# Attention with one key head: early 32-query blocks trade places, outputs take high heads first

## What is computed

```python
xn = layernorm(x, g_in)                                  # x: 64 x 128 x 512
q = heads(xn @ Wq) * 64 ** -0.5                          # 16 heads of 64
k, v = split(xn @ Wkv)                                   # one head of 64
sim = q @ [null_k, k].T + [null_bias, bias]              # 128 x 129 per head
sim = where(causal and mask, sim, -big)
out = softmax(sim) @ [null_v, v]                         # 128 x 64 per head
x + layernorm(concat(out) @ Wo, g_out)
```

## Time and profile before

| | |
|---|---|
| median of 3 runs | 1065.65 us (1062.91 to 1068.68) |
| the profiled execution | 1064.88 us |
| its span | 1063.0 us |
| busy: PE, PEld | 1029.5 us (97%), 902.9 us (85%) |
| busy: DVE, ACT, POOL | 765.8 us (72%), 661.2 us (62%), 828.9 us (78%) |
| TensorE's clock, mean | 0.989 of full |
| chain of work that ended last | PE 89%; projections 38%, outputs 33%, scores 9%, values 9% |

### The profile page before, as it was taken

One profiled execution on the slowest core, in us unless ns is written; L12 is line 12 of the kernel. 1 busy time (PEld: TensorE's weight loads), 2 busy tenths in 40 slices (PEclk: granted clock), 3 DMA queues, 4 the chain that ended last, 5 costly groups with the idle time before them and its releaser, 6 DMA issues.

```text
span 1063.0 us, 42980 instructions
## 1 busy us (share of the span) xinstructions
PE 1029.5 (97%) x14254; PEld 902.9 (85%) x14254; DVE 765.8 (72%) x3513; ACT 661.2 (62%) x2620; POOL 828.9 (78%) x1488
## 2 busy tenths in 40 slices
PE   6789999999999999999999999999999999999986
PEld 6678898888888888888888888888888889889875
DVE  4777777777777777786777787776777777777663
ACT  5655675666675665675665676565676565666552
POOL 2867887778878778878778788788788778787775
PEclk8999999999999999999999999999999999999998
DMA  7312222232222222222223122223222223121101
GB/s 213 124 34 86 77 81 89 67 94 76 63 85 82 74 87 73 68 84 85 76 82 91 50 87 84 86 70 89 62 78 85 83 73 93 54 84 59 50 25 60
DMA packets 90013, 84.01 MB, mean 79 GB/s; under 512 B 21568, under 2 KB 64064, under 8 KB 89792
## 3 DMA queue, kind: packets, MB, share of 16 engines
q1 hardware_dynamic: 88336, 81.03, 25.3%
q10 hardware_dynamic: 1456, 0.04, 0.1%
HBM read 40.11 MB, written 16.78 MB: 54 GB/s over the span
## 4 chain that ended last, share of the span: by engine, by line
PE 89%; issue 2%; POOL 2%; ACT 2%; DVE 1%; POOLq 0%; DVEq 0%; ACTq 0%
PE ps_proj L500 38%; PE ps_pv L488 33%; PE ps_s L452 9%; PE ps_pv L477 9%; ACT exp_bot L914 1%; POOL w_nrm L1112 1%; ACT exp_top L914 1%; POOL y_out L1156 0%; POOL y_nrm L1152 0%; DVE logit_bot L608 0%; DVE o_lo L630 0%; POOL bias_b L1103 0%; ACT xn L942 0%; POOL small L1138 0%; DVE wt L624 0%
## 5 line engine op out<-in xcount | busy, mean ns | idle before, releaser
L914 ACT ACTIVATE exp_bot<-logit_bot,neg_max 128x129 f32<-128x129 f32 x512 | 201.6, 399 | 252.0 <-DVE neg_max L608 223.0
L1103 POOL TENSOR_TENSOR bias_b<-bias_c,mask_add 128x256 f32<-128x256 f32 (+1 forms) x512 | 291.9, 599 | 45.3 <-DVE neg_max L608 45.2
L500 PE MATMUL ps_proj<-xt_hi,wq_hi 128*128 128x256 f32 x1024 | 302.5, 295 | 7.5 <-DVE q_sb L690 6.0
L500 PE MATMUL ps_proj<-xt_lo,wq_hi 128*128 128x256 f32 x1024 | 288.6, 282 | 0.9 <-issue 0.9
L500 PE MATMUL ps_proj<-xt_hi,wq_lo 128*128 128x256 f32 x1024 | 288.6, 282 | 0.0
L608 DVE CUSTOM_DVE_ANT_0 logit_bot<-ps_s,bias_b 128x128 f32<-128x128 f32 x512 | 128.3, 288 | 180.1 <-PE ps_s L452 162.4
L500 PEld LDWEIGHTS ps_proj<-xt_hi,wq_hi 128*128 128x128 f32 x1024 | 193.3, 189 | 24.9 <-issue 13.0
L1112 POOL TENSOR_TENSOR w_nrm<-exp_bot,w_inv 128x256 f32<-128x256 f32 x256 | 156.9, 613 | 65.2 <-DVE w_inv L617 65.2
L488 PE MATMUL ps_pv<-wo_hi,o_hi 128*128 128x512 f32 x488 | 199.0, 408 | 1.2 <-DVE o_lo L630 1.2
L488 PE MATMUL ps_pv<-wo_lo,o_hi 128*128 128x512 f32 x488 | 193.5, 397 | 0.0
L500 PEld LDWEIGHTS ps_proj<-xt_hi,wq_lo 128*128 128x128 f32 x1024 | 193.4, 189 | 0.0
(11 more groups left out here) (94 smaller groups left out, 1778.6 us busy)
## 6 DMA issues: line engine op xcount, KB each, us to landing
x_in<-in_x_dram SPq DMA_DIRECT2D x32, 512.0 KB, 4.1
x_res<-in_x_dram SPq DMA_DIRECT2D x64, 256.0 KB, 2.9
out_dram<-y_out SPq DMA_DIRECT2D x64, 256.0 KB, 2.1
x_split<-xn SPq DMA_DIRECT2D x480, 32.0 KB, 1.9
v_rep<-v_raw SPq DMA_DIRECT2D x256, 32.0 KB, 1.9
w_raw<-in_L_cond_Wq_dram SPq DMA_DIRECT2D x4, 512.0 KB, 11.7
w_raw<-in_L_cond_Wo_dram SPq DMA_DIRECT2D x4, 512.0 KB, 5.2
mask_u<-in_mask_BxS_bk_dram SPq DMA_DIRECT2D x31, 32.0 KB, 3.7
```

The source lines that it names most:

```text
L500: mm = pe.matmul(ps[:, 0:TOK], w[:, k, cols], xt[:, slot, k], start=(j == 0), stop=(j == len(todo) - 1))
L914: ins = nc.scalar.activation(out_[:, s, j], in_[:, s, j], ACT.Exp, bias=neg_max[:, s, k:k + 1], scale=-1.0, accum_out=w_sum[:, s, k:k + 1])
L1103: ins = nc.gpsimd.tensor_tensor(out_, bias, key_mask, ALU.add)
```

## The change

**Blocks trade places.** The tokens of a batch get a new order on chip: block 1 (tokens 32 to 63), block 0, block 2, block 3. TensorE's turning of x becomes a matrix product with placing, an identity whose first two column blocks are exchanged; split_x writes to PLACED[a]. Keys, queries and all that follows are then in this order, so in the early half the even row groups hold tokens 32 to 63 and the odd ones 0 to 31. The early products that need two key blocks move to the even row groups: ITEMS becomes five and five. The masks and the bias follow: mask_of writes two pieces, a second mask causal_early is built, make_bias reads a raw copy of the bias (loaded into the q_sb slot of the second group) and writes bias_c in exchanged order, in four calls of five operations in place of two of four; VectorE's first copy to that q_sb slot waits until all are done. The bias comes in 12 DMAs in place of 8, and every residual load and every store becomes three DMAs of 32, 32 and 64 rows in place of one.

**Outputs.** In each half the eight products with o_hi come first, then the four with o_lo. The half starts when two o_hi and one o_lo of it are made (the bank must be free), and waits for its second o_lo ahead of the four last products.

**Warm-up and layout.** The 30 transposes become three fp32 products of the identity with itself repeated four times, 512 columns wide. A tensor of 32 bytes per partition that nothing uses, home, is allocated ahead of Wo; placing (512 bytes) lies ahead of Wq.

```diff
-WARM = 30
+WARM = 3
+PLACED = (1, 0, 2, 3)
 ITEMS = (
-    [(1, 0), (1, 1), (1, 2), (0, 0)],
-    [(1, 0), (1, 1), (1, 2), (1, 3), (0, 0), (0, 1)],
+    [(1, 0), (1, 1), (1, 2), (0, 0), (0, 1)],
+    [(1, 0), (1, 1), (1, 2), (1, 3), (0, 1)],
 )
+        placing = sb("placing", [P, P])
+        home = sb("home", [P, 8])
         wo_hi, wo_lo = sb("wo_hi", [P, OT, DIM], F32R), sb("wo_lo", [P, OT, DIM], F32R)
+        causal_early = sb("causal_early", [P, HALF])
+        def placed(rows):
+            return ((rows[0:BLK], slice(BLK, HALF)), (rows[BLK:HALF], slice(0, BLK)), (rows[HALF:N], slice(HALF, N)))
             def load_res(q, i):
-                sp.dma_start(x_res[:, i % GB], x_pairs[q, :, i, :]).then_inc(ld_res[i % GB], 16)
+                for rows, at in placed(x_pairs[q, :, i, :]):
+                    sp.dma_start(x_res[at, i % GB], rows).then_inc(ld_res[i % GB], 16)
-                        sp.dma_start(x_split[BLK * r:BLK * (r + 1), :, a],
+                        sp.dma_start(x_split[BLK * r:BLK * (r + 1), :, PLACED[a]],
-                sp.dma_start(out_pairs[p + back // (2 * GB), :, back % (2 * GB), :], y_out[:, b]).then_inc(stored[b], 16)
+                for rows, at in placed(out_pairs[p + back // (2 * GB), :, back % (2 * GB), :]):
+                    sp.dma_start(rows, y_out[at, b]).then_inc(stored[b], 16)
                 hi, lo = heads_of(batch)
-                todo = [(o, w, c) for c in range(CB) for o, w in ((hi, wo_hi), (hi, wo_lo), (lo, wo_hi))]
-                wait(pe, o_lo_made, 4 * batch + 2 + 2 * u)
+                todo = [(hi, w, c) for c in range(CB) for w in (wo_hi, wo_lo)] + [(lo, wo_hi, c) for c in range(CB)]
+                wait(pe, o_hi_made, 4 * batch + 2 + 2 * u)
+                wait(pe, o_lo_made, 4 * batch + 1 + 2 * u)
                 for j, (o, w, c) in enumerate(todo):
+                    if j == 2 * CB:
+                        wait(pe, o_lo_made, 4 * batch + 2 + 2 * u)
-                        mm = pe.transpose(ps[:, N * j:N * (j + 1)], xn[:, b, P * k:P * (k + 1)], ident[:])
+                        mm = pe.matmul(ps[:, N * j:N * (j + 1)], xn[:, b, P * k:P * (k + 1)], placing[:],
+                                       start=(j == 0), stop=(j == KX * GB - 1))
                 pe.wait_ge(ident_made, 1)
+                pe.wait_ge(placing_made, 2)
+                four = ident[:].unsqueeze(1).to_broadcast([P, 4, P])
                 for _ in range(WARM):
-                    pe.transpose(ps_s[0][:, 0:P], ident[:], ident[:])
+                    pe.matmul(ps_s[0][:].rearrange("p (i n) -> p i n", i=4), ident[:], four, start=True, stop=True)
-                nc.vector.tensor_scalar(mask_add[:, k], mask_u8[:, k], MASKED, -MASKED, ALU.mult,
-                                        ALU.add).then_inc(mask_made, 1)
+                nc.vector.tensor_scalar(mask_add[:, k, :, 0:HALF].rearrange("p b (a j) -> p b a j", j=BLK),
+                                        early_swapped(mask_u8[:, k, :, 0:HALF]), MASKED, -MASKED, ALU.mult, ALU.add)
+                nc.vector.tensor_scalar(mask_add[:, k, :, HALF:N], mask_u8[:, k, :, HALF:N], MASKED, -MASKED,
+                                        ALU.mult, ALU.add).then_inc(mask_made, 1)
+            def make_bias(c):
+                null = nb_row[:, c].unsqueeze(2).to_broadcast([P, 2, HALF])
+                null_blocks = nb_row[:, c].unsqueeze(2).unsqueeze(3).to_broadcast([P, 2, 2, BLK])
+                raw_late, raw_early = bot_top(bias_raw[:, c])
+                late, early = bot_top(bias_c[:, c])
+                nc.gpsimd.tensor_tensor(late[:, :, 0:HALF].rearrange("p e (a j) -> p e a j", j=BLK),
+                                        early_swapped(raw_late[:, :, 0:HALF]), null_blocks,
+                                        ALU.subtract).then_inc(bias_made, 1)
+                nc.gpsimd.tensor_tensor(late[:, :, HALF:N], raw_late[:, :, HALF:N], null,
+                                        ALU.subtract).then_inc(bias_shifted, 1)
+                nc.gpsimd.tensor_tensor(early.rearrange("p e (a j) -> p e a j", j=BLK), early_swapped(raw_early),
+                                        null_blocks, ALU.subtract).then_inc(bias_shifted, 1)
+                pool.wait_ge(bias_shifted, 2 * c + 2)
+                for own, mask_ in ((late[:, :, HALF:N], causal), (early, causal_early)):
+                    nc.gpsimd.tensor_tensor(own, own, mask_[:].unsqueeze(1).to_broadcast([P, 2, HALF]),
+                                            ALU.add).then_inc(bias_made, 1)
+                pool.wait_ge(bias_made, 3 * c + 3)
+                dve.wait_ge(bias_made, 3 * CB)
                 q_copies(1, 0)
                 make_bias(0)
+                make_bias(1)
                 bias(0)
                 bias(1)
-                make_bias(1)
+                make_bias(2)
+                make_bias(3)
                 x_rstd_of(1)
```

More of the change, by code:

```diff
@@ L180, in attention_block @@
         causal_zero, causal_made = sem("causal_zero"), sem("causal_made")
+        early_zero = sem("early_zero")
+        placing_made, early_filled = sem("placing_made"), sem("early_filled")
         filled = sem("filled")
@@ L209, in attention_block @@
         last_g_made, last_out_made = sem("last_g_made"), sem("last_out_made")
-        COL_LOADS, ROW_LOADS, BIAS_LOADS, V_LOADS = 4, 2, 8, 8
+        COL_LOADS, ROW_LOADS, BIAS_LOADS, V_LOADS = 4, 2, 12, 8
+        bias_raw = q_sb[:, 1].rearrange("p c u n -> p (c u n)")[:, 0:CB * (BOT + TOP)].rearrange(
+            "p (c n) -> p c n", c=CB)
+        PIECES = 3
         SPLITS = (N // BLK) * (P // BLK)
@@ L369, in _ @@
             for b in range(GB):
-                sp.sem_inc(stored[b], 16)
+                sp.sem_inc(stored[b], 16 * PIECES)
             load_x(0, 0)
@@ L380, in _ @@
                 for e in range(2):
-                    sp.dma_start(bias_c[up, :, N * e:N * (e + 1)], by_head[u, e, HALF:N]).then_inc(ld_bias, 16)
-                    sp.dma_start(bias_c[up, :, BOT + HALF * e:BOT + HALF * (e + 1)],
-                                 by_head[u, e, 0:HALF, :, 0:HALF]).then_inc(ld_bias, 16)
+                    sp.dma_start(bias_raw[up, :, N * e:N * (e + 1)], by_head[u, e, HALF:N]).then_inc(ld_bias, 16)
+                    for a in range(2):
+                        row = HALF * u + BLK * PLACED[a]
+                        sp.dma_start(bias_raw[row:row + BLK, :, BOT + HALF * e:BOT + HALF * (e + 1)],
+                                     by_head[u, e, BLK * a:BLK * (a + 1), :, 0:HALF]).then_inc(ld_bias, 16)
             load_x(0, 1)
@@ L432, in _ @@
             for b in range(GB):
-                sp.wait_ge(stored[b], 16 * GROUPS + 16)
+                sp.wait_ge(stored[b], 16 * PIECES * (GROUPS + 1))
         @block.tensor
@@ L696, in _ @@
             nc.vector.memset(logit_top[:, :, :, HALF:HALF + 1], 0.0).then_inc(filled, 1)
+            dve.wait_ge(ident_made, 1)
+            nc.vector.tensor_copy(placing[:].rearrange("p (a j) -> p a j", j=BLK)[:, 0:2],
+                                  ident[:].rearrange("p (a j) -> p a j", j=BLK)[:, 1::-1]).then_inc(placing_made, 1)
+            nc.vector.tensor_copy(placing[:, HALF:N], ident[:, HALF:N]).then_inc(placing_made, 1)
             x_stats_of(0, 0)
@@ L1153, in residual @@
                 wait(pool, y_g_made, batch + 1)
-                wait(pool, ld_res[b], stored_before(batch, b) + 16)
-                wait(pool, stored[b], stored_before(batch, b) + 16)
+                wait(pool, ld_res[b], stored_before(batch, b) + 16 * PIECES)
+                wait(pool, stored[b], stored_before(batch, b) + 16 * PIECES)
                 nc.gpsimd.tensor_tensor(y_out[:, b], y_nrm[:, b], x_res[:, b], ALU.add).then_inc(y_out_made, 1)
             def stored_before(batch, b):
-                return 8 * (batch - b)
+                return 8 * PIECES * (batch - b)
             nc.gpsimd.memset(ident[:], 0.0).then_inc(ident_zero, 1)
@@ L1171, in _ @@
             pool.wait_ge(causal_made, 2)
+            nc.gpsimd.memset(causal_early[:], 0.0).then_inc(early_zero, 1)
+            pool.wait_ge(early_zero, 1)
+            for u in range(2):
+                row = HALF * u + BLK
+                nc.gpsimd.memset(causal_early[row:row + BLK, 0:BLK], -MASKED).then_inc(early_filled, 1)
+            pool.wait_ge(early_filled, 2)
+            for g in range(P // BLK):
+                row, h = BLK * g, g % 2
+                own = causal_early[row:row + BLK, BLK * h:BLK * (h + 1)]
+                nc.gpsimd.affine_select(out=own, in_=own, compare_op=ALU.is_ge, fill=-MASKED, base=0,
+                                        pattern=[[-1, BLK]], channel_multiplier=1).then_inc(early_filled, 1)
@@ L1172, in _ @@
+            pool.wait_ge(early_filled, 6)
             pool.wait_ge(filled, 1)
             x_rstd_of(0)
-            def make_bias(i):
-                cs = slice(2 * i, 2 * i + 2)
-                for k, part in enumerate((bias_c[:, cs, 0:BOT], bias_c[:, cs, BOT:])):
```

(11 more changed lines are left out.)

6 lines of the change are left out of this document (4 added, 2 removed).

## The result

The changed kernel takes 1079.4 us (median of 13 runs, 1071.1 to 1088.8); the kernel before took 1066.1 beside it (13 runs, 1061.2 to 1068.7). The ratio is 1.0119, 95% interval 1.0094 to 1.0143, where 1056 us was forecast. Two of the 13 runs (1087.5 and 1088.8 us) were in a slower state of the chip and are not in the ratio; the median of the other 11 is 1078.9. The profiled execution of the changed kernel took 1081.0 us, span 1079.2.

What follows compares the result with a forecast made beforehand. TensorE was taken as the bound, busy 898.8 of 900 us. Span 1063.0 - 11.6 (values) - 7.7 (outputs) + 5 (pieces) + 4.5 (start) + 0.4 (rest) = 1053.6; runs' median 2.65 above, so 1056 us, range 1042 to 1068.

Steps and rivals of the forecast that it cites:

- Three pieces per store and per residual load: SP's queue: eight more DMAs per group of two at 0.54 us each delay the x_in load; +5 us.
- a load 2.9 us late, a pitch of 0.67: x_in load on SP: the point where a body's loss passes its gain of 1.3 us.
- SP becomes the path: Rival, SP's queue: at 0.76 us per piece +30 us in place of +5, so 1081 us; chance 0.10.
- The room: Slack of the x_in load before VectorE's x_stats: 3.2 us, 2.3 at the worst, taken as 2.8.
- 0.3 reaches TensorE: Start of each of 15 bodies: x_in 1.9 us late, 1.6 absorbed, 0.3 left for TensorE.
- The values: Value products in five rounds for all groups: 0.19 us less per call, 61 calls, -11.6 us.
- Issue sets the values calls: Rival, values calls: 80 records take what they took, so no -11.6 and 1068 us; chance 0.10.
- The outputs: Entry into the output projection, high heads first: the 0.18 us bubble goes; -7.7 us (-4.7 to -9.3).
- The tie: Output entries where ScalarE's chain does not move along: first o_lo at 538.52 plus 0.05 against TensorE's 538.59.
- The start: Before the loop: fp32 turning of x, bias loads and make_bias operations cost +4.5 us (+2 to +8).
- Addresses: Wo and all behind it move: term zero; rival with 2 ns per matmul, 1046 or 1066 us, chance 0.10.
- if TensorE waits over 1.3 us per body: Falsifying sign: TensorE waits longer per body than the gain of 1.3 us from values and outputs.

Runs made afterwards that it cites:

- experiment 7: The changed kernel with only the residual loads as whole transfers again, stores still in three pieces: 1051.1 us, ratio 0.9867 to the kernel before.
- experiment 1: The changed kernel with the loads of x_in and its mask issued earlier, right behind the previous group's 16 splits: 1045.0 us, ratio 0.9809 to the kernel before.
- experiment 12: The kernel before with the outputs' new order, the early x_in load and 14 warm-up transposes in place of 30: 1053.7 us, ratio 0.9861.
- experiment 10: Experiment 1's kernel with the outputs' old order and old single wait put back: 1062.7 us, ratio 0.9979 to the kernel before.
- experiment 8: Experiment 1's kernel without the 32 unused bytes (home) ahead of Wo: 1044.8 us beside 1045.0.
- experiment 2: The changed kernel with each store and residual load as one transfer of 128 rows again: 1045.0 us, ratio 0.9803 to the kernel before.
- experiment 6: The kernel before with stores and residual loads in three pieces and the x_in load issued early: 1064.7 us, ratio 0.9994.
- experiment 5: The kernel before with the outputs' new order and the early x_in load: 1062.8 us, ratio 0.9974.
- experiment 11: Experiment 5's kernel with 46 warm-up transposes in place of 30, TensorE's later code 32 instructions further on: 1110.4 us, ratio 1.0415 to the kernel before.
- experiment 9: Experiment 1's kernel with a sixth round of value products put back: 1080.8 us, ratio 1.0150 to the kernel before.

## Why the prediction was wrong

**The step that failed** is "*Three pieces per store and per residual load*", in its price: "The pieces go between SBUF and HBM like that pair: I take 0.54". From one issue to the next, the changed kernel's 32-row stores take 0.53 us (median), its 64-row stores 0.75, the 32-row residual loads 0.62, and from the 64-row one to whatever follows 1.02, where the whole load took 0.79. A store with its load went from 0.55 + 0.79 to 1.80 + 2.26 us: 2.7 us more for four more transfers, 0.68 each, and 5.4 per group of two. The whole stretch grew by 5.9 and 6.4, because v_rep and x_split also took longer at times; why wasn't settled. Forecast was 4.3. Ahead of the group whose room was worked out it was 5.9; with 0.7 of shorter interval and 2.8 of room the load is 3.8 us late by the prediction's own sum, not 1.9, and in the trace x_stats wait 3.3 us for it on average there. The text's own point of decision, "a load 2.9 us late, a pitch of 0.67", was passed, and its rival *SP becomes the path* gave 1081 for a measured 1079.4. That it came so close is in part luck: it had 0.76 per piece and 2.0 us lost per body, where 0.68 and 2.8 were measured, and gains smaller than the measured ones. (By the text's own terms the load at 0.76 is 3.7 us late, not 3.6.) The room was read to within half a microsecond: in experiment 7, 3.1 us longer, the load is 1.0 us late by the same sum and 1.4 in the trace, less than the 1.6 that VectorE absorbs, and only 2.4 us in all reach TensorE. A chance of 0.10 for a case that 0.13 us per transfer decides was too little, the more so as the text named the sign for it (32 partitions, like those that cost 0.63 to 0.76).

**What it cost, by terms.** From the sixth group's x_stats to the thirtieth's, twelve bodies, the trace has 760.5 us before, 777.6 after and 743.5 in experiment 1. The loss is 34.1 us, 2.8 per body, where "0.3 reaches TensorE" was forecast. Of these, 2.0 are the waits on q_sb from start to start (1.8 as the profile counts them, 25.1 us over 13.9 bodies), and 0.6 the lower clock beside the long ones (five falls, four of them measured, at 1.3 to 2.6 us each); some 0.2 are not traced. The clock was in no term of the sum.

**The values** were right. Forecast -11.6; in the call 0.21 us x 61 = 12.9, and between experiments 12 and 1, which differ in them, the pieces and the start, 752.4 - 743.5 = 8.9 us for 48 calls, 11.3 for 61. The rival *Issue sets the values calls* is out, and with it a floor on the distance of starts: 80 records start within 1.16 us, 15 ns apart. By the 25 ns of the Trainium skill's "TensorE: Matmul & The Clock Gate", section "Wait, 56ns, not 53.3ns?", it would be an estimated 2.0 us.

**The outputs** were undersized. Forecast -7.7; experiment 12 against before is 8.1 us in twelve bodies with 48 outputs, 10.3 for 61. The tie that the text feared in every second batch does not occur: 1 to 4 late entries of 61 without stalls, in the changed kernel 14. That the term depends on the values was seen, but only for the new order; experiment 10 shows the larger effect on the old one.

**The start** was oversized. Forecast +4.5; the fifth group's x_stats begin at 85.75 us where they began at 84.30, and in the experiments with the same start 0.3 to 3.5 us later than before. **Addresses** were rightly zero (experiment 8). Put together for experiment 1, where x_stats run 3.0 us late when the steady bodies begin: 1063.0 - 11.3 - 10.3 + 3.0 = 1044.4, against a span of 1044.9. The terms come from the same traces, so this shows that nothing is left over, and is no test of each.

**Signs that were named.** SyncE's longer stretch (4.3 forecast, 5.9 to 6.4 seen), x_stats waiting for x_in (2 us forecast at every second group; 3.3 there, 2.5 over all 20 waits, up to 5.1) and TensorE's wait on q_sb behind it all appeared; "if TensorE waits over 1.3 us per body" was the named falsifier and is what happened.

By the page "DMA: Bandwidth & Descriptors" of the Trainium skill, section "Rules for kernel authors", many small transfers are to be coalesced into one; the bound that it names is 64 KB, and the pieces are 64 and 128 KB. Coalescing does take the loss away here (experiment 2, 1045.0 us). But experiment 6 has all the pieces and loses nothing, since no later transfer is late: the count alone is not what costs.

Still open: why single issues on SyncE take over 1 us now and then, and why the instruction packets arrive at different times from body to body, so that experiment 5 waits in some bodies and not in others.

## What to carry to other kernels

When a change adds transfers to a queue, take for each edge the room of the tightest load behind it and ask at which price per transfer it is used up; if the rows hold prices on both sides of that point, as 0.54 and 0.63 to 0.76 did here, the loss is a main case and not a tail. The remedy is seldom fewer transfers: issue the load that somebody waits for ahead of those that nobody waits for (1079.4 to 1045.0 us with the same transfers). And before a few microseconds are put down to an edit of TensorE's program, look for idle on "issue" at one fixed product of the loop: shifts of 32 instructions, one either way, put the same kernel 9 us below and 48 us above.

## What the runs showed of the hardware

Issue time on SyncE differed by shape: a store of 32 or of 128 rows of 2 KB was followed by the next issue after 0.53 to 0.55 us, one of 64 rows after 0.75. A long stall costs TensorE more than itself: after 3.35 us nearly without work its granted clock was 0.57 for 3.9 us, and stalls of 3.2 to 3.7 us cost 1.3 to 2.6 us each on top. And supply of instructions can bound a loop of small products: TensorE's instructions came in blocks of 256, and at one border of a block per body it stood 1.8 to 2.9 us when the border fell into a values call (experiment 11; 0.4 to 1.0 us in experiment 9), 0.3 to 2.3 us in some bodies when it fell two products behind one, and not at all 16 products further into the projection.
